# Moving the four-row softmax of 16 tiles off the tensor engine, in an attention layer on one core

## The reference

```python
x  = hidden_states                            # 4 batches, 1024 rows, 512 columns, float32
xn = layernorm(x)
w_cmp   = softmax((xn @ Wcmp + bcmp).reshape(B, 256, 4))            # over each group of 4 rows
entries = einsum('bcr,bcrh->bch', w_cmp, xn.reshape(B, 256, 4, 512))
ck = rope(rmsnorm(entries @ Wk + bk));  cv = entries @ Wv + bv      # 256 compressed keys, values
q  = rope(rmsnorm(xn @ Wq + bq));  lk = rope(rmsnorm(xn @ Wlk + blk));  lv = xn @ Wlv + blv
# 16 heads: the 8 best compressed keys of each row, and a local window of 128 + 128 rows
out = (sparse(q, ck, cv) + local(q, lk, lv)) * 0.5 @ Wo + bo
ffn = dequant(fp8(xn * s0)) @ dequant(fp8(W2 * s1))
return x + out + ffn
```

## Time and profile before

| what | value |
|---|---|
| runs of before | 2493.33 us median of 3 (2492.55 to 2494.22) |
| profiled execution | span 2492.2 us, from its first to its last instruction; no time of its own beside it is given |
| PE, PEld | 99%, 88% busy |
| DVE, ACT, POOL | 80%, 67%, 70% busy |
| DMA | 232 MB, 93 GB/s |
| granted PE clock | 1.000 over the span |

### The profile page before, as it was taken

The page is one execution under the profiler, slowest core; times in us unless marked ns, Lnnn a source line. Parts: engine busy times, 40 slices in busy tenths (PEclk is TensorE's granted clock), DMA queues, the critical chain, the costliest instruction groups (busy, mean ns, idle before and its releaser), DMA issues. The chain is left out here.

```text
span 2492.2 us, 56206 instructions
## 1 busy us (share of the span) xinstructions
PE 2462.4 (99%) x15574; PEld 2190.6 (88%) x15606; DVE 1996.7 (80%) x6637; ACT 1675.3 (67%) x4866; POOL 1749.7 (70%) x3150
## 2 busy tenths in 40 slices
PE   7999999999999999999999999999999999999998
PEld 6888888888888988888888889888888888888887
DVE  7788888888778887787777888887878878888786
ACT  5667777767666677667666666767676666666665
POOL 6787787776786666666677766666667767676674
PEclk9999999999999999999999999999999999999999
DMA  5433233333332122121441221221235213212301
GB/s 159 136 107 113 71 109 115 117 109 117 123 119 82 52 90 90 60 90 43 151 150 53 81 82 60 90 86 64 78 124 166 94 59 100 75 61 94 98 10 52
DMA packets 183530, 232.36 MB, mean 93 GB/s; under 512 B 19762, under 2 KB 101172, under 8 KB 183220
## 3 DMA queue, kind: packets, MB, share of 16 engines
q1 hardware_dynamic: 182644, 228.50, 28.3%
q10 hardware_dynamic: 576, 0.26, 0.1%
HBM read 162.64 MB, written 65.01 MB: 91 GB/s over the span
## 5 line engine op out<-in xcount | busy, mean ns | idle before, releaser
L1598 POOL TENSOR_TENSOR t<-raw,tB 128x128 f32<-128x128 f32 x512 | 226.4, 464 | 593.8 <-DVE raw L1167 593.7
L987 ACT ACTIVATE ch<-bVC,blT 128x128 fp32r<-128x128 f32 x512 | 160.5, 365 | 511.1 <-PE bVC L726 511.1
L631 PE MATMUL bQK<-wh,xh 128*128 128x512 f32 x1024 | 424.4, 414 | 0.0
L632 PE MATMUL bQK<-wl,xh 128*128 128x512 f32 x1024 | 403.8, 394 | 0.0
L633 PE MATMUL bQK<-wh,xl 128*128 128x512 f32 x1024 | 401.4, 392 | 0.0
L1542 POOL TENSOR_TENSOR r<-ss,mh 128x4 f32<-128x4 f32 x256 | 286.4, 1119 | 60.1 <-DVE ss L1175 57.5
L647 PE MATMUL bVC<-wh,xh 128*128 128x256 f32 x1024 | 310.0, 303 | 0.0
L954 ACT ACTIVATE P<-P,nm,r 128x256 f32<-128x256 f32 (+1 forms) x512 | 295.3, 583 | 0.0
L1203 DVE CUSTOM_DVE_ANT_0 P<-bS,cst 128x256 f32<-128x256 f32 (+1 forms) x512 | 204.2, 399 | 110.5 <-PE bS L679 106.1
L649 PE MATMUL bVC<-wh,xl 128*128 128x256 f32 x1024 | 289.4, 283 | 0.0
L648 PE MATMUL bVC<-wl,xh 128*128 128x256 f32 x1024 | 289.0, 282 | 0.0
(11 more groups left out here) (188 smaller groups left out, 7617.9 us busy)
## 6 DMA issues: line engine op xcount, KB each, us to landing
wh<-kept SPq DMA_DIRECT2D x144, 256.0 KB, 4.1
wl<-kept SPq DMA_DIRECT2D x144, 256.0 KB, 4.6
kept<-wh SPq DMA_DIRECT2D x48, 256.0 KB, 3.2
kept<-wl SPq DMA_DIRECT2D x48, 256.0 KB, 3.4
woh<-kepto SPq DMA_DIRECT2D x48, 256.0 KB, 3.2
wol<-kepto SPq DMA_DIRECT2D x48, 256.0 KB, 3.7
ini<-in_hidden_states SPq DMA_DIRECT2D x24, 256.0 KB, 4.5
xs<-xsh SPq DMA_DIRECT2D x24, 256.0 KB, 2.5
```

The lines of the kernel that those rows point to most:

```text
L631: e.matmul(bQK[:, :], a, b, start=kt == 0, stop=False)
L632: e.matmul(bQK[:, :], a, bl, start=False, stop=False)
L1598: last = e.tensor_tensor(t2[:, :, :, d_], raw[:, u % 2, :, :, s_], tB[:, :, u % 8, d_].unsqueeze(1).broadcast_to([128, 2, 2, 32]), ALU.mult)
```

## The change

For tiles 16 to 31 the logits leave PE. The 128 logits (one a partition) go to DRAM and come back as a 32x4 tile (`spread`, `gather`: two transfers); DVE, ACT and DVE make the softmax of the four (`below_max`, `exp_4`, `shares`); the 32x4 weights go to DRAM and come back as 128x128, the same in all partitions (`give`, `widen`). POOL adds the two parts of the turned tile (`whole_x`), multiplies by the weights (`weigh`) and adds the columns by four into `et` (`fold`, two instructions). The four transfers are issued at the end of SP's step. `logits`, `group_max`, `exp_w`, `weights4`, `entries` and `put_et` are gone for these tiles.

The product of the feed-forward of tile t now alternates with the turns of tile t+1 (`turn_ffn`), which stand ahead of the scores. So `tile_base` is 4 steps earlier, and `ffn_base(t)` is `tile_base(t + 1)`, 7 steps after the tile's own base, where it was 5. The last tile of a batch keeps a product of its own. The rest (`XR` 3 instead of 4, semaphores merged) makes room for buffers and semaphores.

```diff
 def tile_base(t):
-    return t - AHEAD if t < 8 else 14 + 6 * (t - 8) if t < 16 else 64 * (t // 8 - 1) + 9 + 7 * (t % 8)
+    return t - AHEAD if t < 8 else 14 + 6 * (t - 8) if t < 16 else 64 * (t // 8 - 1) + 5 + 7 * (t % 8)
...
-LAGS = {"stats": (0, 0, 0), "power": (0, 0, 0), "norm": (1, 1, 1), "turn": (2, 2, 3), "hi": (2, 2, 3), "lo": (2, 2, 3),
-        "max": (2, 2, 3), "ew": (3, 3, 4), "wm": (3, 3, 4), "et": (3, 4, 8), "park": (3, 3, 4)}
+LAGS = {"stats": (0, 0, 0, 0), "power": (0, 0, 0, 0), "norm": (1, 1, 1, 1), "turn": (2, 2, 3, 3), "hi": (2, 2, 3, 3),
+        "lo": (2, 2, 3, 3), "max": (2, 2, 3, None), "ew": (3, 3, 4, None), "wm": (3, 3, 4, None), "et": (3, 4, 8, None),
+        "park": (None, None, 4, 4), "spread": (None, None, None, 2), "gather": (None, None, None, 3),
+        "below": (None, None, None, 4), "share": (None, None, None, 5), "give": (None, None, None, 6),
+        "widen": (None, None, None, 7), "whole": (None, None, None, 5), "weigh": (None, None, None, 8),
+        "fold": (None, None, None, 10)}
-BLOCK_LAGS = {"kv": (4, 5, 7), "put": (4, 5, 7), "rope": (4, 5, 7), "turn": (6, 6, 9), "hi": (6, 6, 9), "lo": (6, 6, 9)}
+BLOCK_LAGS = {"kv": (4, 5, 7, 11), "put": (4, 5, 7, 11), "rope": (4, 5, 7, 11), "turn": (6, 6, 9, 13), "hi": (6, 6, 9, 13),
+              "lo": (6, 6, 9, 13)}
...
 def ffn_base(t):
-    return 64 * (NB - 1) + 2 + 7 * t // 2 if t < NL else tile_base(t) + 5
+    if t < NL:
+        return 64 * (NB - 1) + 2 + 7 * t // 2
+    return tile_base(t) + 6 if t % 8 == 7 else tile_base(t + 1)
...
+            def spread(t):
+                e.wait_ge(S["wl"], t + 1)
+                e.dma_start(spread_l[t].rearrange("(p a) -> p a", a=1), smt[:, t % 2, 2:3]).then_inc(S["d_g0"], 16)
+            def gather(t):
...
+                e.wait_ge(S["d_g0"], 16 * (n + 1))
+                e.dma_start(l4, spread_l[t].rearrange("(g r) -> g r", r=4)).then_inc(S["d_g1"], 16)
+            def give(t):
+                e.wait_ge(S["wq"], 2 * n + 2)
+                e.dma_start(spread_w[t].rearrange("(g r) -> g r", r=4), w4).then_inc(S["d_g2"], 16)
+            def widen(t):
...
+                e.wait_ge(S["d_g2"], 16 * (n + 1))
+                e.dma_start(wide[:, :], bc(spread_w[t], 128)).then_inc(S["d_g3"], 16)
...
-            def entries_ffn(t, f):
-                e.wait_ge(S["wm"], t + 1)
+            def turn_ffn(t, f):
+                e.wait_ge(S["xn"], t + 1)
                 e.wait_ge(S[free["T"][0]], free["T"][1])
                 e.wait_ge(S["q8"], 4 + ffn_pos(f) + 1)
                 e.wait_ge(S[free["Y"][0]], free["Y"][1])
                 for kt in range(KT):
                     c = slice(kt * 128, (kt + 1) * 128)
-                    m = e.matmul(entries_of(t)[:, kt * 32:(kt + 1) * 32], xt[:, t % XR, c], wm[:, :], start=True, stop=True)
+                    m = e.transpose(bT[:, c], xt[:, t % XR, c], ident)
...
+            def exp_4(t):
+                e.wait_ge(S["lm"], 2 * n + 2)
+                e.activation(e4, l4, ACT.Exp, accum_out=sum4).then_inc(S["lw"], 1)
...
+            def below_max(t):
+                e.wait_ge(S["d_g1"], 16 * (n + 1))
+                e.tensor_reduce(top4, l4, mybir.AxisListType.X, ALU.max).then_inc(S["lm"], 1)
+                e.tensor_scalar(l4, l4, top4, None, ALU.subtract, ALU.bypass).then_inc(S["lm"], 1)
+            def shares(t):
+                e.reciprocal(inv4, sum4).then_inc(S["wq"], 1)
+                e.tensor_scalar(w4, e4, inv4, None, ALU.mult, ALU.bypass).then_inc(S["wq"], 1)
...
+            def whole_x(t):
+                e.wait_ge(S["lo_x"], t + 1)
+                e.tensor_tensor(xf[:, :, :], f32(xsh[:, :, :]), f32(xsl[:, :, :]), ALU.add).then_inc(S["xf"], 1)
+            def weigh(t):
+                e.wait_ge(S["d_g3"], 16 * (n + 1))
+                w = wide[:, :].unsqueeze(1).broadcast_to([128, KT, 128])
+                e.tensor_tensor(xf[:, :, :], xf[:, :, :], w, ALU.mult).then_inc(S["xf"], 1)
+            def fold(t):
+                e.tensor_tensor(x4[:, :, 0:2], x4[:, :, 0:2], x4[:, :, 2:4], ALU.add).then_inc(S["xf"], 1)
+                e.wait_ge(S["kv"], t // 4)
+                e.tensor_tensor(et[:, :, (t % 4) * 32:(t % 4 + 1) * 32], x2[:, :, :, 0], x2[:, :, :, 1],
+                                ALU.add).then_inc(S["put_et"], 1)
```

More of the change, by code:

```diff
@@ L25 @@
 SQD = float(D) ** 0.5
-XR, QR = 4, 2
+XR, QR = 3, 2
 C_ID, C_MK, C_MG, C_SEL, C_M32, C_N = 0, 128, 512, 640, 672, 704
@@ L43 @@
     "kscale hi_qk pl hi_p lo_p lo_cv sq el es put_v hi_c wohi hi_x b8 ew put_et css hi_ck c8 "
-    "lo_qk rs raw t1 krest add ngr mc m8 ttr mr nm lo_c acc wolo bs ba xv xn wl dg lo_x "
-    "eg re wm init nb cke cm crest cadd cks lo_ck bl rsc isc wk tab ctab rs0 "
[2 rows of a table removed]
+    "lo_qk rs raw t1 krest add ngr mc m8 ttr mr nm lo_c acc wolo xv xn wl dg lo_x "
+    "eg re wm init nb cke cadd cks lo_ck bl isc wk tab ctab rs0 "
[2 rows of a table added]
     "d_r0 d_r1 d_r2 d_r3 d_r4 d_r5 d_r6 d_r7 "
@@ L109, in block_at @@
         late = 2 if k >= 2 and k % 2 == 0 else 0
-        if tile_base(4 * k + 3) + BLOCK_LAGS[stage][min(k, 2)] + late == s:
+        if tile_base(4 * k + 3) + BLOCK_LAGS[stage][min(k, 2) + (4 * k >= NL)] + late == s:
             return k
@@ L556, in run_sync @@
                     double(2 * (s // 64 + 1))
-                if s >= 64 and s % 64 == 2 and s < NU:
+                if s >= 64 and s % 64 == 3 and s < NU:
                     double(2 * (s // 64) + 1)
@@ L594, in run_sync @@
                     load_ini(t)
+                if tile_at(s, "widen") is not None:
+                    widen(tile_at(s, "widen"))
+                if tile_at(s, "give") is not None:
+                    give(tile_at(s, "give"))
+                if tile_at(s, "gather") is not None:
+                    gather(tile_at(s, "gather"))
+                if tile_at(s, "spread") is not None:
+                    spread(tile_at(s, "spread"))
             for u in range(NU - 7, NU):
@@ L841, in run_tensor @@
                     fill(8)
-                if tile_at(s, "turn") is not None:
+                beside = tile_at(s, "turn") is not None and ffn_at(s, 3) is not None
+                if beside:
+                    turn_ffn(tile_at(s, "turn"), ffn_at(s, 3))
+                elif tile_at(s, "turn") is not None:
                     turn_x(tile_at(s, "turn"))
@@ L850, in run_tensor @@
                     ckv(block_at(s, "kv"))
-                if tile_at(s, "et") is not None and ffn_at(s, 3) is not None:
-                    entries_ffn(tile_at(s, "et"), ffn_at(s, 3))
-                elif tile_at(s, "et") is not None:
+                if tile_at(s, "et") is not None:
                     entries(tile_at(s, "et"))
-                elif ffn_at(s, 3) is not None:
+                if ffn_at(s, 3) is not None and not beside:
                     ffn(ffn_at(s, 3))
@@ L859, in run_tensor @@
                     values(u4, 1)
-                if tile_at(s, "turn") is not None:
-                    logits(tile_at(s, "turn"))
+                if tile_at(s, "max") is not None:
+                    logits(tile_at(s, "max"))
                 if u0 is not None:
@@ L1094, in run_scalar @@
                     exp_w(tile_at(s, "ew"))
+                if tile_at(s, "share") is not None:
+                    exp_4(tile_at(s, "share"))
                 if block_at(s, "hi") is not None:
@@ L1127, in run_scalar @@
                         hi_wo(q)
-                if tile_at(s, "norm") is not None:
+                if tile_at(s, "norm") is not None and tile_at(s, "norm") < NL:
                     diagonal(tile_at(s, "norm"))
@@ L1458, in run_vector @@
                     group_max(tile_at(s, "max"))
+                if tile_at(s, "below") is not None:
+                    below_max(tile_at(s, "below"))
                 if u0 is not None:
@@ L1484, in run_vector @@
                     weights4(tile_at(s, "wm"))
+                if tile_at(s, "share") is not None:
+                    shares(tile_at(s, "share"))
                 if block_at(s, "rope") is not None:
@@ L1705, in run_gpsimd @@
                     power_x(tile_at(s, "power"))
+                if tile_at(s, "whole") is not None:
+                    whole_x(tile_at(s, "whole"))
+                if tile_at(s, "weigh") is not None:
+                    weigh(tile_at(s, "weigh"))
+                if tile_at(s, "fold") is not None:
+                    fold(tile_at(s, "fold"))
                 if s >= 0:
```

98 lines of the change are left out of this document (71 added, 27 removed), and 4 rows, old and new, of the table SIGNALS.

## The result

| | median | runs |
|---|---|---|
| before | 2493.11 us | 4, 2492.55 to 2494.22 |
| changed | 2509.09 us | 4, 2507.82 to 2510.87 |

The account below looks back on a forecast made before the run. PE was taken to bound the kernel. Shed work -15.5, pile +24, fold +5.4 and `init` +0.7 made +14.6 us on the span of 2492.2; with runs 1.1 above the span, about 2508 us, range 2485 to 2518.

Parts of the forecast that it names:

- What bounds it: PE, 99% busy almost without waits: work it sheds is won in full, waits it gets are lost in full.
- What PE sheds: Logits, entries, some waits and cheaper transposes leave PE's time: 15.5 us won (14.0 to 16.2).
- The fourth: Transposes alternated with bf16 products on PE cost 0.33 us instead of 0.44: 1.5 us won over 14 (0 to 2.2).
- The pile: DVE gets 5.15 us extra in two steps in a row per tile; PE waits, mostly at `turn_ffn`: 24 us (14 to 31).
- `init` before the output projection: On DVE `lo_x` and `init` stand together, so L742 may wait for `init` where `lo_x` comes last: 0.7 us, residue 4.
- The fold: POOL's fold is late for `ckv` in steps 129 and 193; PE waits 2.7 us each, 5.4 us (4.6 to 7.8).
- Transfers at 0 (0 to 2): The four new transfers on SP's queue hold up nothing due within a step: 0 us, bounds 0 and 2.
- (1): DVE's idle time takes up the pile, all but some 2 us: 2486 us, chance 0.18.
- (2): DVE's idle time takes up the pile and the fold is in time too: 2480 us, chance 0.04.
- (3): The pile is half absorbed, 10 to 14 us of waits, change and losses cancel: 2488.3 to 2498.3 us, chance 0.11.
- (4): POOL's new instructions also hold DVE up, 0.5 us a tile, 7 us more: 2515 us, chance 0.12.
- the 2525: Time if the shared DVE and GpSimd port lock makes `excess`'s third instruction wait behind a whole `weigh`, up to 1.2 us a tile.

Follow-up runs that it names:

- f3: e4 with logits sent straight from SBUF to SBUF and the fold of tiles 23 and 31 one step earlier: 2482.01 us.
- f4: e1 with logits sent straight from SBUF to SBUF and the fold of tiles 23 and 31 one step earlier: 2485.95 us.
- e3: Changed kernel with the feed-forward product back behind the scores, alone, the turns alone ahead of them, DVE's pile kept: 2500.25 us.
- g3: Changed kernel with `excess` alone one step earlier, so DVE's extra work lies in three steps in a row: 2502.54 us.
- g1: Changed kernel with the logits going straight from SBUF to SBUF, without 4-byte writes to DRAM: 2510.10 us.
- e1: Changed kernel with `excess` and `rejoin` of the 16 late tiles two steps earlier on DVE, so the pile is apart: 2496.39 us.
- e4: Changed kernel with `ffn_base` back at `tile_base` + 5 for late tiles, so the product alternates with nothing: 2497.20 us.
- g2: Changed kernel with POOL's `weigh` one step later for every late tile: 2511.31 us.

## Why the prediction was right

**What bounds it** was right: all that moved came from PE's waits and PE's work, with nothing caught up.

**What PE sheds:** 15.5 us said, 13.9 measured: steps 64 to 199 are 16.2 us longer in all, and the terms below make 30.1 of that. The terms read from rows held: a step that had the pair is 1.40 to 1.45 us shorter in every kernel (step 180, 1.25 to 1.29), a product alone costs 0.88 (read as 0.86 from the earlier trace rows). The fourth, 1.5 us for transposes at 0.33 us beside bf16 products, was mis-sized: they take 1.31 - 0.88 = 0.43, against 0.45 alone, 0.3 us for all 14. The bound of nothing was near the truth; the row taken for nearest, alternated `entries`, has 32 columns a pass and not 128. f3 is 12.6 us shorter than before in the same steps.

**The pile:** 24 us said, 22 measured, tile by tile within 0.6 us. The absorption read from brackets in plain steps was a good measure. What the prediction took for one cause was two that work together. The same tiles without the pile (f4) still cost 2.1 us a batch, since `turn_ffn` stands where q8 has only 0.46 us in reserve; with the pile but the product back behind the scores (e3) they cost 5.9; in f3, with neither, nothing. Of the 22 us, some 6 come only where both meet. That the sizes agree so well is in part luck: the table has nothing for the place by itself, and its own figures fit a pile of three steps worse (g3). Tiles 19 and 20 stand 0.07 and 0.12 us above what its rule gives, and its test, 1.8 us of `excess` that arrive as 1.3, says that residue 4 absorbs 0.5 and not 0.35.

The wait for q8 is where it was forecast. POOL's `quant_nan` is named in 9 of 14 steps and `add_out` in 2 (114 and 178). In 107 no releaser is named, in 100 and 164 (residue 4) the wait is too short for the list; but there too PE starts 0.26 us after `quant_nan` ends, as in the nine. Step 100:

```profile
985.37 0.40 PE L684 MATMUL bQK<-wh,xh 128*128 128x512 f32 x1
...
985.60 1.17 POOL L1723 TENSOR_TENSOR q<-q,qn 128x512 bf16<-128x512 bf16 x1
...
987.03 0.62 PE L839 MATMUL bT<-cst,xt 128*128 128x128 f32 x2
...
991.28 0.74 DVE L1442 SCALAR_TENSOR_TENSOR ini<-bY,isc,ini 128x512 f32<-128x512 f32 x1
...
992.17 0.47 PE L795 MATMUL bY<-woh,ch 128*128 128x512 f32 x1
```

So 12 of the 14 waits are for q8. The 0.13 us added for the semaphore fits where PE follows DVE (0.11 to 0.15); behind `quant_nan` it is 0.26. Steps 100 and 164 are the same in f4: for tile 20 all 0.6 us are the place's, none the pile's. The wait for `lo_p` came in step 85 (0.57 us) and, with no releaser named, in 106 (0.30; `lo_p` ends 0.11 us before the product starts); in 92 it was for `lo_c` at L700 (0.32), not foreseen.

**`init` before the output projection:** 0.7 us said for residue 4, 0.3 in each of steps 100 and 164 measured. L795 starts 0.15 us after `init` ends in the timeline above, 0.66 behind the transposes of q and k where f3 has 0.38. These 0.6 us stand in the table under tile 20, so inside the 22.

**The fold:** 2 x 2.7 said, 2 x 2.1 measured (the two instructions of the fold take 0.61 and 0.41, where 0.74 and 0.46 were estimated, and POOL is through `normalise_p` 0.3 us sooner). The clock's 3.2 us in step 129 were in no term. So 5.4 and 7.4, inside the bound of 7.8 for another reason than the one given.

**Transfers at 0 (0 to 2):** right in the sum and wrong in the reason. Step 69 is 0.9 us longer, where `load_ini` of tile 16 (256 KB) now stands on SP right ahead of `fetch_wo`; in g1, with the same order there, it is 0.1, so this is chance in part. And the statement that nothing is due within a step overlooked `fetch_wo`, whose landing PE wants 9 us after it may start. The spread costs up to 5 us in each of two steps, the fall of the clock included; the pile hid it. With the pile gone it showed at once (e1), and at full size with an earlier PE (e4).

**Sum:** -13.9 + 22.0 + 4.2 + 3.2 + 0.7 = +16.2 in steps 64 to 199; the rest of the spans' difference of 16.5 lies outside them. Said were +14.6. The terms are off by +1.6 (shed), -2.0 (pile), -1.2 (fold) and, the largest, +3.2 (clock), and the 0.7 us said are `init`'s while the 0.7 measured are step 69's: part of the closeness is luck. The mechanism is not: the waits stand where they were forecast.

**Rivals.** (1) and (2) fall by the table, and (3), which wanted 10 to 14 us of waits, by its 22. (4) wanted 0.5 us a tile more than the sum; the tiles came out 2 us below it, and `excess`'s third instruction has a mean of 0.74 us, against 0.77 before. With that falls the 2525 that the Trainium skill ("SBUF — State Buffer", Who interferes with whom) would allow: no run here shows its lock to cost this kernel anything beyond the mean durations.

## What to carry to other kernels

To price work put on an engine that isn't the bottleneck, don't use its busy share: read from brackets how much idle each kind of step has, and carry the backlog from step to step until the bound engine meets it. That gives the size, not each part: here it was good to 10% for the change and 25% low for g3. When a loss is removed, look for what it had hidden: here 22 us of stalls covered up to 10 us of transfers, and only a run with the idea alone, and what the transfers and the fold cost mended (f3), showed that it was worth 11 us. A tiny transfer can be dear for others: keep single elements out of neighbouring places in DRAM.

## What the hardware showed that was not expected

- 128 writes of 4 bytes into 512 bytes of DRAM: for 7 to 10 us after them 256 KB transfers move at 30 GB/s, single packets taking up to 8.6 us. With the logits 64 bytes apart, or from SBUF to SBUF, the longest takes 2.2 us, `give`'s 32 writes of 16 bytes into 512 bytes included.
- The granted clock after a wait of 1.85 us at `ckv` (2.1 in g2) fell to 0.50 in 7 of 18 such waits (nine kernels, two each), in step 129 or 193 or both, and cost 3.2 us or 1.6 us; in the other 11 it stayed. Both waits of e4 for the output weights (3.0 and 3.3 us) were followed by such a fall, and none of the waits of 1.8 us at `turn_ffn` in steps 93 and 157 (changed kernel, g1, g3). In e1, step 193 (waits of PE, then the granted clock):

```profile
1872.04 2.51 PE L861 MATMUL bY<-wkv,et 128*128 128x256 f32 x7 [1.85 <-POOL et L1751]
```

```profile
1871.00:1873.00 2.00, 0.96 (x4) 0.98 0.93 265
1873.00:1875.00 2.00, 2.00 (x6) 0.50 0.85 269
```

What decides between the two is open. It may account for part of the spread of a kernel's times: with both waits e1's runs reach from 2493.3 to 2497.6 us, without them f3's from 2481.6 to 2482.5. But f4's, also without them, reach from 2485.2 to 2488.0, so it isn't all.
